# One written order per engine for a whole recurrent stage, its turned outputs in another PSUM bank, the gate's weights loaded first

## What is computed

```python
# block 1: recurrent, chunks of 64 tokens, 4 heads; B=2, T=1024
q, k, v = x @ Wq, x @ Wk, x @ Wv                 # 128, 128, 256 columns, x layer-normalised
g = log_sigmoid(x @ Wgk1 @ Wgk2 + bgk2) / 16     # Wgk1 is 128x16, Wgk2 is 16x128
def step(S, inp):
    qg = qb * exp(bb) * scale; kd = kb * exp(-bb)          # bb = cumsum of g in the chunk
    A = tril(qg @ kd.T)
    o = A @ vb + qg @ S
    S = S * exp(b_last) + (kb * exp(b_last - bb)).T @ vb
    return S, o
o = o * rsqrt(mean(o*o) + EPS) * rms_w * silu(x @ Wg)
x1 = x + layernorm(o @ Wo)
# block 2, twice: h = shift(x); x += local_attention(h @ wqkv) @ wo
#                 h = layernorm(shift(x)); x += (a * gelu(g)) @ w2 + b2, with a, g = split(h @ w1 + b1)
out = x1 + layernorm(block2(layernorm(x1)))
```

## Time and profile before

| | |
|---|---|
| time before, median of 3 runs | 438.07 us (437.63 to 439.78) |
| the profiled execution's own time | 437.89 us |
| its span, first to last instruction | 435.7 us |
| mean granted TensorE clock | 0.995 |
| busy PE / DVE / ACT / POOL | 407.0 / 339.8 / 303.3 / 292.6 us |

### The profile page before, as it was taken

The page is one execution under the profiler, slowest core; times in us unless marked ns, Lnnn a source line. Parts: engine busy times, 40 slices in busy tenths (PEclk is TensorE's granted clock), DMA queues, the critical chain, the costliest instruction groups (busy, mean ns, idle before and its releaser), DMA issues.

```text
span 435.7 us, 13201 instructions
## 1 busy us (share of the span) xinstructions
PE 407.0 (93%) x4851; PEld 291.6 (67%) x4851; DVE 339.8 (78%) x720; ACT 303.3 (70%) x677; POOL 292.6 (67%) x287
## 2 busy tenths in 40 slices
PE   3898999879999999999999999999999999999993
PEld 2566666656776877777766666668777777776563
DVE  3678867889888989989845377898899899865676
ACT  2677768758877887887773346778878878865322
POOL 3578967899978788777723536677777777761425
PEclk9999999999999999999999999999999999999998
DMA  7830000000000000000000000000000000000012
GB/s 191 307 92 3 2 3 3 3 1 2 8 14 9 9 11 10 8 11 11 8 9 13 0 2 1 8 9 8 11 11 8 11 12 8 7 10 13 10 32 62
DMA packets 21038, 10.37 MB, mean 24 GB/s; under 512 B 13236, under 2 KB 20208, under 8 KB 20976
## 3 DMA queue, kind: packets, MB, share of 16 engines
q1 hardware_dynamic: 20400, 9.14, 7.6%
q10 hardware_dynamic: 576, 0.39, 0.3%
HBM read 6.38 MB, written 1.05 MB: 17 GB/s over the span
## 4 chain that ended last, share of the span: by engine, by line
PE 66%; issue 7%; DVE 5%; POOL 5%; ACT 5%; DVEq 0%; ACTq 0%; POOLq 0%
PE psum L628 49%; PE psum L900 6%; PE psum L942 5%; PE psum L967 4%; ACT sq L1368 1%; PE psum L873 1%; ACT probs_t L1400 1%; POOL ping L446 1%; DVE o_n L1964 1%; POOL qr L475 1%; POOL qr L483 1%; ACT qk_t L1387 1%; DVE neg_max L1937 1%; PE psum L987 1%; POOL zn L511 1%
## 5 line engine op out<-in xcount | busy, mean ns | idle before, releaser
L475 POOL TENSOR_TENSOR qr<-rot 128x1024 f32<-128x1024 f32 x32 | 75.8, 2370 | 26.9 <-DVE rot L1909 22.2
L628 PE MATMUL psum<-wqkv_sb,h_t 128*128 128x512 f32 x192 | 93.0, 594 | 0.0
L483 POOL TENSOR_TENSOR qr<-qr,inv 128x1024 f32<-128x1024 f32 x32 | 60.8, 1902 | 33.7 <-ACT inv L1379 33.6
L1917 DVE TENSOR_REDUCE ss<-sq 128x16 f32<-128x1024 f32 x32 | 39.0, 1219 | 14.9 <-ACT sq L1368 14.7
L1393 ACT ACTIVATE probs<-probs 128x512 f32<-128x512 f32 x64 | 39.4, 631 | 13.9 <-DVE probs L1944 13.5
L1937 DVE TENSOR_REDUCE neg_max<-psum 128x4 f32<-128x512 f32 x64 | 41.5, 684 | 7.2 <-PE psum L628 5.8
L628 PE MATMUL psum<-z_t,w_sb 128*128 128x512 f32 (+1 forms) x96 | 44.7, 595 | 0.0
L628 PEld LDWEIGHTS psum<-wqkv_sb,h_t 128*128 128x128 f32 x192 | 31.7, 191 | 16.3 <-issue 16.2
L1944 DVE TENSOR_TENSOR probs<-psum,neg_max 128x512 f32<-128x512 f32 x64 | 41.3, 680 | 0.2
L1909 DVE TENSOR_TENSOR rot<-psum,cos_t 128x1024 f32<-128x1024 f32 x32 | 39.1, 1222 | 2.7 <-PE psum L628 2.4
L900 PEld LDWEIGHTS psum<-consts,qr 128*128 128x128 f32 x256 | 29.6, 141 | 16.6 <-POOL qr L483 13.1
(11 more groups left out here) (150 smaller groups left out, 964.4 us busy)
## 6 DMA issues: line engine op xcount, KB each, us to landing
wqkv_sb<-in_L_ffn_wqkv SPq DMA_DIRECT2D x1, 1536.0 KB, 10.1
hcat<-middle SPq DMA_DIRECT2D x32, 32.0 KB
out_x<-pong SPq DMA_DIRECT2D x8, 128.0 KB, 1.8
hcat<-middle SPq DMA_DIRECT2D x32, 31.8 KB
x_in<-in_L_attn_x SPq DMA_DIRECT2D x2, 384.0 KB, 4.4
w_sb<-in_L_ffn_w SPq DMA_DIRECT2D x1, 682.0 KB
cos_base<-rotary_cos SPq DMA_DIRECT2D x1, 512.0 KB, 5.6
sin_base<-rotary_sin SPq DMA_DIRECT2D x1, 512.0 KB, 7.1
```

What stands on the lines that cost most here:

```text
L475: pool.tensor_tensor(o, a, b[:, :, ::-1, :], ALU.add).then_inc(s["add_ready"], 1)
L483: pool.tensor_tensor(a, a, inv[:, :].unsqueeze(2).to_broadcast([P, 2 * AH, DH]), ALU.mult).then_inc(s["qr_ready"], 1)
L628: return pe.matmul(o, w, m, start=start, stop=stop, skip_group_check=skip)
L1917: dve.tensor_reduce(ss[:, 0:4 * AH:2], sq[:, :].rearrange("p (h e) -> p h e", e=DH), AX.X, ALU.add).then_inc(s["ss_ready"], 1)
```

## The change

It has five parts.

1. `gla_step` and `attention_beside_last_pairs` are gone on all four engines. In their place `recurrent_stage_and_first_tiles` writes out every step from pair 0 to attention tile 2, on each engine its own list.
2. `transpose_o` writes bank 3 instead of banks 6 and 7. `intra_outputs` no longer waits for `ogt_ready`; `transpose_o(t)` waits until `project_vg(t+1)` has been read by both its readers, and `project_vg(t)` waits until the turned outputs of pair t-2 have been copied. The attention's `project_v`, which uses bank 3 too, gets such waits in the list.
3. The combining of the gate's weights moves to bank 7, and the wait for it from `transpose_x(0)` to `project_gate(0)`.
4. DMAs: Wgk1 and Wgk2 are issued first on ACT's queue, Wv and Wg take their places on SP's.
5. Pairs 0 and 1 are normalised by DVE (`normalise_first`) instead of POOL.

```diff
@@ sync @@
-            sp.dma_start(wgk1_sb[:, :], Wgk1).then_inc(d["d_low"], 16)
-            sp.dma_start(wgk2_sb[0:RANK, :], Wgk2).then_inc(d["d_low"], 16)
+            sp.dma_start(wvg_sb[:, 0:GV], Wv).then_inc(d["d_vg"], 16)
+            sp.dma_start(wvg_sb[:, GV:2 * GV], Wg).then_inc(d["d_vg"], 16)
@@ scalar @@
+            act.dma_start(wgk1_sb[:, :], Wgk1).then_inc(d["d_low"], 16)
+            act.dma_start(wgk2_sb[0:RANK, :], Wgk2).then_inc(d["d_low"], 16)
             act.dma_start(wqk_sb[:, 0:P], Wq).then_inc(d["d_qk"], 16)
             act.dma_start(wqk_sb[:, P:2 * P], Wk).then_inc(d["d_qk"], 16)
-            act.dma_start(wvg_sb[:, 0:GV], Wv).then_inc(d["d_vg"], 16)
-            act.dma_start(wvg_sb[:, GV:2 * GV], Wg).then_inc(d["d_vg"], 16)
@@ vector @@
+            def normalise_first(t):
+
+                dve.wait_ge(s["x_rstd"], t + 1)
+                for b in range(B):
+                    at = t * B + b
+                    ins = dve.tensor_scalar(xn[:, at * P:(at + 1) * P], tile_of(x_in, at), mv_x[:, 2 * at:2 * at + 1],
+                                            rstd_x[:, at:at + 1], ALU.subtract, ALU.mult)
+                ins.then_inc(s["xn_ready"], 1)
@@ tensor @@
             def project_vg(t, par):
                 wait(pe, s["xnt_ready"], t + 1)
                 wait(pe, s["v_ready"], t)
                 wait(pe, s["gin_ready"], t)
+                wait(pe, s["ogt_ready"], t - 1)
...
             def intra_outputs(t, par):
...
                 wait(pe, s["og1_ready"], t)
-                wait(pe, s["ogt_ready"], t)
...
             def transpose_o(t, par):
                 wait(pe, s["og2_ready"], t + 1)
+                wait(pe, s["v_ready"], min(t + 2, NP))
+                wait(pe, s["gin_ready"], min(t + 2, NP))
                 for i in range(2 * B):
-                    ins = pe.transpose(bank[6 + i // 2][:, HC + i % 2 * P:HC + (i % 2 + 1) * P],
+                    ins = pe.transpose(bank[3][:, i * P:(i + 1) * P],
                                        og2[:, par * VW + i * P:par * VW + (i + 1) * P], ident)
@@ tensor, the new list, its first pairs @@
+                    transpose_x(0, 0)
+                    project_gate(0, 0)
+                    project_vg(0, 0)
+                    transpose_x(1, 1)
+                    gla_project_qk(0, 0)
+                    project_gate(1, 1)
+                    project_vg(1, 1)
+                    intra_scores(0, 0)
+                    transpose_x(2, 0)
+                    transpose_kd(0, 0)
+                    gla_project_qk(1, 1)
+                    project_gate(2, 0)
+                    key_values(0, 0)
+                    intra_outputs(0, 0)
+                    state_outputs(0, 0)
+                    intra_scores(1, 1)
+                    transpose_kd(1, 1)
+                    gla_project_qk(2, 0)
+                    key_values(1, 1)
+                    intra_outputs(1, 1)
+                    gla_transpose_o(0, 0)
+                    state_outputs(1, 1)
+                    project_out(0, 0)
+                    project_vg(2, 0)
+                    intra_scores(2, 0)
+                    transpose_x(3, 1)
+                    transpose_kd(2, 0)
+                    gla_transpose_o(1, 1)
+                    project_gate(3, 1)
+                    intra_outputs(2, 0)
+                    key_values(2, 0)
+                    project_out(1, 1)
+                    gla_project_qk(3, 1)
+                    state_outputs(2, 0)
+                    project_vg(3, 1)
...
@@ vector, the new list, its start @@
+                    stats_x(0, 0)
+                    aggregate_x(0, 0)
+                    copy_gate_weights()
+                    stats_x(1, 1)
+                    aggregate_x(1, 1)
+                    normalise_first(1)
+                    decay_min(0, 0)
+                    stats_x(2, 0)
+                    aggregate_x(2, 0)
+                    gate_input(0, 0)
+                    decay_cumulate(0, 0)
...
+                    state_1(0, 0)
+                    decay_min(2, 0)
+                    gate_input(1, 1)
+                    sum_o(0, 0)
+                    mask_scores(1, 1)
...
@@ gpsimd, the lists around attention tiles 0 to 3 @@
+                    normalise_f(3, 1)
+                    normalise_f(4, 0)
                     gate_values(6, 0)
                     gate_o(6, 0)
                     add_y(5, 1)
-                    normalise_f(3, 1)
+                    rotate_add(0, 0)
                     second_state(7, 1)
-                    rotate_add(0, 0)
                     gate_values(7, 1)
                     scale_qk(0, 0)
-                    gate_o(7, 1)
                     rotate_add(1, 1)
-                    add_y(6, 0)
-                    scale_qk(1, 1)
                     mix_values(0, 0)
                     keep_values(0, 0)
-                    normalise_f(4, 0)
+                    gate_o(7, 1)
+                    scale_qk(1, 1)
+                    add_y(6, 0)
+                    rotate_add(2, 0)
                     normalise_f(5, 1)
-                    rotate_add(2, 0)
-                    scale_qk(2, 0)
-                    normalise_f(6, 0)
-                    add_y(7, 1)
                     mix_values(1, 1)
                     keep_values(1, 1)
+                    normalise_f(6, 0)
+                    scale_qk(2, 0)
+                    add_y(7, 1)
                     rotate_add(3, 1)
+                    normalise_f(7, 1)
                     scale_qk(3, 1)
-                    normalise_f(7, 1)
```

More of the change, by code:

```diff
@@ L448, in normalise_f @@
                 ins.then_inc(s["xf_ready"], 1)
[L450 to L461, removed]
             for l in range(DEPTH):
@@ L770, in project_out @@
                 ins.then_inc(s["y_done"], 1)
-            def gla_step(k, par):
-                paired(project_vg, k, 0)
-                paired(transpose_x, k, 1)
-                paired(intra_scores, k, 0)
-                paired(project_gate, k, 1)
-                paired(transpose_kd, k, 0)
-                paired(project_qk, k, 1)
-                paired(transpose_o, k, -1)
-                paired(key_values, k, 0)
-                paired(project_out, k, -1)
-                paired(intra_outputs, k, 0)
-                paired(state_outputs, k, 0)
             combine_gate_weights()
-            iterate(pe, gla_step, first=-3, end=FREE_PAIR)
             gla_project_qk, gla_transpose_o = project_qk, transpose_o
@@ L1037, in drain, with recurrent_stage_and_first_tiles @@
                     transpose_z(last, 1)
-                def attention_beside_last_pairs():
+                def recurrent_stage_and_first_tiles():
+                    transpose_x(0, 0)
[33 more added lines that the diff above has]
+                    project_vg(3, 1)
+                    transpose_x(4, 0)
+                    intra_scores(3, 1)
+                    project_gate(4, 0)
+                    transpose_kd(3, 1)
+                    gla_project_qk(4, 0)
+                    intra_outputs(3, 1)
+                    key_values(3, 1)
+                    gla_transpose_o(2, 0)
+                    state_outputs(3, 1)
+                    project_out(2, 0)
@@ L1040, in attention_beside_last_pairs @@
                     project_vg(4, 0)
+                    intra_scores(4, 0)
                     transpose_x(5, 1)
-                    intra_scores(4, 0)
+                    transpose_kd(4, 0)
+                    gla_transpose_o(3, 1)
                     project_gate(5, 1)
-                    transpose_kd(4, 0)
-                    project_vg(5, 1)
-                    gla_transpose_o(3, 1)
+                    intra_outputs(4, 0)
+                    key_values(4, 0)
                     gla_project_qk(5, 1)
@@ L1060, in attention_beside_last_pairs @@
                     project_out(4, 0)
-                    intra_outputs(5, 1)
+                    project_vg(6, 0)
                     state_outputs(5, 1)
@@ L1076, in attention_beside_last_pairs @@
                     transpose_in(0, 0)
-                    key_values(6, 0)
-                    intra_outputs(6, 0)
+                    gla_transpose_o(5, 1)
                     state_outputs(6, 0)
-                    pe.wait_ge(s["ht_ready"], 1)
+                    transpose_in(1, 1)
+                    project_vg(7, 1)
+                    pe.wait_ge(s["ht_ready"], 2)
                     project_out(5, 1)
@@ L2053, in attention_beside_last_pairs @@
-                    state_1(4, 0)
-                    gate_input(5, 1)
-                    sum_o(4, 0)
-                    stats_x(7, 1)
+                    stats_f(2, 0)
                     scale_o(4, 0)
                     mask_scores(5, 1)
-                    aggregate_x(7, 1)
+                    aggregate_f(2, 0)
+                    gate_input(5, 1)
+                    decay_min(6, 0)
                     state_0(5, 1)
-                    decay_min(6, 0)
-                    stats_f(3, 1)
```

526 lines of the change are left out of this document (338 added, 188 removed).

## The result

The changed kernel takes 457.11 us (median of 4 runs, 456.57 to 459.67) against 438.73 for the kernel before beside it: a ratio of 1.044 (95% interval 1.041 to 1.047). It is slower by 18.4 us, and the forecast was a gain of 4.4. Span of the profiled run: 454.9 us, before 435.7.

What follows compares the result with a forecast made beforehand. PE was taken to bound the kernel, some 8.8 us a pair, with DVE close under it. Gains of 2.3 + 0.7 + 0 + 1.4 = 4.4 us gave 433.5, against the median 433.7; forecast 433.6, range 430.0 to 438.8.

Steps and rivals of the forecast that it cites:

- Head: Start up to `project_vg(2)`: weights first, bank 7, DVE normalising, new first list; 2.3 us gained (bounds 1 and 3.6).
- the sign: Sign of a right mechanism at the start: the scan of pair 0 still starts past 12 us.
- Middle, pairs 2 and 3: From `project_vg(2)` to `project_vg(4)`: three PE waits lose their reasons, 19.0 instead of 19.70 us; 0.7 us gained.
- 1.20 us a pair: PE's waits in the middle: `key_values` 0.60, `project_out` 0.33, `state_outputs` 0.27 us; the gain there is up to this.
- (a): Rival: PE's order closes all holes, pairs 2 and 3 take 8.9 us each; 431.5 us, chance 0.22.
- Pairs 4 to 7: Up to the attention's first `project_qk`, a written list in both kernels: 0 gained (bounds 1.5 gained, 1 lost).
- `project_qk(0)` to `scores(3)`: Last stretch before `scores(3)`, 39.33 us: POOL ends last and its new order gains 1.4 us (bounds 0 and 2.5).
- Behind `scores(3)`: Rest of the program, PE busy 303.9 of 315.0 us: untouched by the change, only shifted along.
- (b): Rival: denser engines collide, DVE's scan and POOL's state product slow each other in four more pairs; 437.2 us, chance 0.12.
- (c): Rival: bank 3 ties pairs together, PE stalls 1.5 us at six `transpose_o`; 442.5 us, chance 0.12 with milder forms.
- (d): Rival: DVE uses up the start's lead in the middle, only the POOL part stays; 436.5 us, chance 0.08.

Runs made afterwards that it cites:

- Experiment 3: The kernel before with only DVE's and ACT's waits for the ten column transfers (d_cols) put ahead of its loop over the pairs: 461.06 us, ratio 1.051.
- experiment 1: The changed kernel with DVE's and ACT's waits for the ten column transfers (d_cols) moved behind the recurrent stage's list: 433.75 us, ratio 0.989 to the kernel before.
- experiment 9: The kernel of experiment 1 with the DMA issues of Wgk1, Wgk2, Wv and Wg in their old order: 435.0 us, ratio 0.994.
- experiments 5 to 7: On the kernel of experiment 1: POOL's normalise_f(7) behind scale_qk(3), 433.71 us; PE's transpose_qk(3) ahead of transpose_o(1), 434.77 us; both edits, 435.49 us.
- experiment 5: The kernel of experiment 1 with POOL's normalise_f(7) moved behind scale_qk(3): 433.71 us, ratio 0.988.
- experiment 8: The kernel of experiment 1 with the turned outputs of pairs 0 to 6 back in banks 6 and 7, and the order this forces: 451.73 us, ratio 1.027.

## Why the prediction was wrong, and where it was right

**The step that failed** is the one that was never taken: the forecast walked through each engine's new list from its first entry, and let that list start at the time at which the old loop starts. The part "Head" counts the moved transfers, and says what is queued behind them on SP and ACT. What stands in program order between the old place and the new one of the stage itself wasn't looked at: one wait on DVE's queue and one on ACT's. So the term for entering the lists was put at nothing, without a reason; it measured 23.8 us at the first `stats_x`. No rival holds it either; all four, the slower one too, were about what happens inside the lists. The range ended 18 us below the result.

Both halves could be read ahead of any run. That there is a wait stands in the code only: it cost nothing before, so no view of waits shows it. What it would cost stands in the trace of the kernel before, where SP issues the last of the ten columns late:

```profile
25.54 0.37 SPq L324 DMA_DIRECT2D columns<-in_L_ffn_b  x1
```

DVE's first `stats_x` starts at 3.53 us there. A transfer issued at 25.54 can't release it before some 26, so at least 22 us were on the table, five times the gain that was being added up in tenths. Experiment 3 has the full price in the kernel before: 24.2 us of span.

**The terms,** read at the marks the forecast named, from the kernel of experiment 1. The timeline of its PE:

```profile
27.96 1.88 PE L647 MATMUL psum<-wvg_sb,middle 128*128 128x512 f32 x4
...
33.47 0.45 PE L647 MATMUL psum<-hid,probs 64*32 64x64 f32 x32
33.86 1.16 PE L647 MATMUL psum<-wout_sb,pong 128*128 128x128 f32 x8
...
44.41 1.00 PE L647 MATMUL psum<-state,middle 32*64 32x64 f32 x32 [0.72 <-issue]
...
46.33 1.88 PE L647 MATMUL psum<-wvg_sb,middle 128*128 128x512 f32 x4
...
77.07 1.96 PE L647 MATMUL psum<-wqkv_sb,h_t 128*128 128x512 f32 x4 [0.17 <-issue]
...
116.45 0.41 PE L647 MATMUL psum<-masks_bf,ident_bf 64*64 64x512 bf16 x4
```

- *Head,* forecast 2.3: `project_vg(2)` at 27.96, forecast 27.9, before 30.18: **2.2**. The first step came at 4.38 (forecast 4.9), the scan of pair 0 at 12.63 (12.4, and past 12 as the sign asked), `state_outputs(0)` at 19.41 (19.35). The walk along the lists was right to a few tenths; what it said of the first microsecond was right only against the kernel before (experiment 9).
- *Middle, pairs 2 and 3,* forecast 0.7: `project_vg(4)` comes 18.37 us behind `project_vg(2)`, before 19.70: **1.3**. `key_values` and `project_out` have no idle time in either pair, where the earlier trace rows had 0.60 and 0.33. But "1.20 us a pair" was read from pair 2 alone: in pair 3 of the kernel before `key_values` (at 45.69 us) has no idle time, only `project_out` and `state_outputs` do (0.30 and 0.27). The stall that the walk put at `state_outputs(3)` is there (0.72, forecast 0.6), the one at `transpose_o(1)` hardly. The two pairs:

```profile
27.95:36.75 8.80, 8.59 (x157) 5.86 (x155) 6.45 (x20) 6.89 (x21) 6.78 (x9) 1.00 0.01 2
36.75:46.33 9.58, 8.69 (x161) 6.23 (x155) 7.81 (x24) 7.56 (x21) 6.38 (x8) 1.00 0.02 4
```

  Pair 2 goes at PE's own pace, as rival (a) had it, pair 3 as before. DVE is busy 6.45 us in pair 2 instead of 8.60: the walk had taken it for full. In pair 3 it isn't full either (7.81 of 9.58). By the times in the trace `state_outputs(3)` comes late because `key_values(3)` (42.64) stands late in PE's list, with only `transpose_o(2)` behind it to cover the state's way over DVE and POOL, which ends at 44.30.
- *Pairs 4 to 7,* forecast 0: 46.33 to 77.07 takes 30.74 us, before 31.48: **0.7**.
- *`project_qk(0)` to `scores(3)`,* forecast 1.4: 39.38 us, before 39.33: **0**. This term failed. "What ends last here is POOL" was read off POOL's busy share, 8.90 of 9.41 us; but the same line of the earlier trace rows has PE busy 9.41 of 9.41, and in the earlier trace rows `transpose_qk(3)` has no idle time ahead of it. PE, not POOL, was full there. The swap did bring `rotate_add(0)` 0.56 us earlier against `project_qk(0)` (4.49 instead of 5.05), and `scores(0)` came no earlier (14.04 us behind `project_qk(0)`, before 14.00). `scale_qk(2)` did end where the forecast had it, 26.75 us behind `project_qk(0)` (forecast 26.5). Behind it POOL waits 0.88 us for the statistics of pair 7, and PE waits for `o_n`, whose cover has moved in PE's new list (experiments 5 to 7):

```profile
107.72 1.57 POOL L443 TENSOR_SCALAR ping<-x_attn,mv_f,rstd_f 128x128 f32<-128x128 f32 x2 [0.88 <-ACT rstd_f L1359]
...
111.07 0.66 PE L975 MATMUL psum<-consts,o_n 128*128 128x128 f32 x4 [0.78 <-DVE o_n L2082]
```

  Relieving POOL (experiment 5) leaves the stretch as long as it was.
- *Behind `scores(3)`,* taken as unchanged: 314.95 us, before 315.01. Right.

The sum is 4.2 us where 4.4 was forecast. That agreement is luck: the errors cancel, 0.6 and 0.7 too little in the middle, 1.4 too much at the end.

**The rivals.** (a) came true in pair 2 and a part of pairs 4 to 7, not as a whole. (b), collisions: the scans take 936 ns on the mean from 12 to 70 us, before 906, so there is no general price. The row on which (b) was built is misread, too. The scan at 37.22 us starts 0.61 us ahead of the state product that was named as its neighbour; what it starts behind is another POOL product of the kernel before:

```profile
37.14 0.73 POOL L373 TENSOR_TENSOR cos_t<-cos_base,scales 128x256 f32<-128x256 f32 x1
```

And the state product is on the way to `state_outputs`, not from the gate to the scores. One scan stands out in the kernel of experiment 1:

```profile
23.28 1.27 POOL L432 TENSOR_TENSOR pong<-z_t 128x512 f32<-128x512 f32 x1 [0.56 <-DVE z_t L1879]
...
23.30 1.79 DVE L1817 TENSOR_TENSOR_SCAN probs<-consts,probs 128x256 f32<-128x256 f32 x1
...
12.63 0.68 DVE L1817 TENSOR_TENSOR_SCAN probs<-consts,probs 128x256 f32<-128x256 f32 x1
```

The scan that starts 0.02 us behind POOL's product takes 1.79 us, the one without such a neighbour 0.68; it is longer by 1.1, and POOL's product has 1.25 to go when it starts. By the rule of the Trainium skill (SBUF — State Buffer, Who interferes with whom), a DVE instruction with two SBUF inputs contends with a GpSimd instruction that reads SBUF for a port pair that is an exclusive lock, and the order of issue decides who is blocked. These rows agree, within 0.15 us. (c), bank 3 as a tie: no wait of over 1 us at `transpose_o` up to `project_qk(0)`, and in experiment 8 these lists are slower without it. (d), the lead not passed on: refuted by the marks, and by experiment 9.

## What to carry to other kernels

When a stage moves to another place in a program, read every instruction and above all every wait that stands between the old place and the new one on each queue, and ask at what time its condition becomes true; a wait that costs nothing in the trace before can cost all of its transfer's lateness when work moves behind it (here 23.8 us). Put a wait for constants right ahead of their first reader. And an engine that is busy nine tenths of a stretch isn't yet its bound: look at whether the other engines wait for it there at all. And when a step moves ahead in a list, ask which wait it covered where it stood.

## What the hardware showed that was not expected

**PE's first matmuls run at half pace while its clock reads full.** In the kernel of experiment 1 the windows' granted clock is 1.00 from the start, yet:

```profile
7.17 1.22 PE L647 MATMUL psum<-middle,wgk_sb 128*128 128x256 f32 x2 [0.47 <-ACT middle L1256]
8.19 3.10 PE L647 MATMUL psum<-wvg_sb,middle 128*128 128x512 f32 x4
...
17.04 0.59 PE L647 MATMUL psum<-middle,wgk_sb 128*128 128x256 f32 x2
```

And in the changed kernel, after its idle time of 23.8 us, with no transfer running (DMA share 0.00 from 28 to 32 us):

```profile
31.61 3.22 PE L647 MATMUL psum<-wvg_sb,middle 128*128 128x512 f32 x4
```

The same two matmuls take 1.22 us early and 0.59 later, `project_vg` 3.10 and 3.22 instead of 1.88. In experiment 8, where the row reads 0.51, the same four take 3.53. So these are the durations of the lower level (1.2 GHz) for the most part. The Trainium skill (TensorE: Matmul & The Clock Gate, What's actually happening) says that TensorE is at the lower level when idle and comes up with work; the durations agree, the clock row does not. Durations of a start must be taken from a start. In experiment 8 the row and the durations agree.

**A short issue isn't always short.** SP takes 0.37 to 0.72 us to issue each of nine of the column transfers in experiment 1, but 1.58 for the third (at 21.41 us); in the changed kernel the fourth takes 1.38, and in the kernel before none took over 0.69. The same last transfer is issued at 25.54, 25.37 and 26.19 us in the kernels before, after and of experiment 1, so in these three runs the time of what stands last in the queue varies by 0.8 us.
